# A Mamba mixer between two half feed-forward layers on one core: order in the first block, roots ahead of states, four banks for turned rows, the two closing items joined, the last product in two parts

## The chip, the cores and the metric

One core of a Trainium2 chip. The metric is the device time of one launch in microseconds (us), as the median of several runs. Engines are named as in the profile: PE (matmuls), PEld (its weight loads), DVE, ACT, POOL, and SP, which here only issues DMAs. The clock of PE has two levels, 1.2 and 2.4 GHz; the profile gives the share that is granted.

## What is computed

The input is 4 batches of 512 tokens with 512 features, in fp32. Three layers follow one another, each with a residual:

```
x = x + 0.5 * ffn(layernorm(x))
x = x + mixer(layernorm(x))
x = x + 0.5 * ffn(layernorm(x))

ffn:   h = fwht(x * SU_ug) / 64
       up   = h @ W_up.T   * scale      (512 -> 2048)
       gate = h @ W_gate.T * scale
       h = fwht(silu(gate) * up * SU_dp) / 64
       return h @ W_down.T * scale      (2048 -> 512)
mixer: gate, xBC, dt = split(x @ in_proj.T)        (512 -> 1024 + 1280 + 64)
       xBC = silu(causal conv of width 4 over time)
       state-space scan in chunks of 64 tokens: 64 heads of 16, state 128
       y = rmsnorm((y + D x) * silu(gate)) @ out_proj.T
```

Both feed-forward layers use the same weights. The Walsh-Hadamard transforms (fwht) are folded into the weights by the kernel itself in its opening part.

## The kernel before, in words

**Precision.** A product of two fp32 matrices is made as three passes over high and low halves (fp32r), so 128 x 128 weights against 512 columns are three matmuls, and a projection over 512 features is 12. Where rows come out of an engine, ACT writes the high half (a copy) and DVE the low half (a subtraction).

**Opening part** (`begin`, to about 363 us): it transforms the weights and runs the first feed-forward layer for batches 0 and 1. The change doesn't touch it.

**Items.** `mixer` then runs six items, q = 0 to 5. In items 0 to 3 the mixer of batch q runs, and beside it a feed-forward layer of another batch, `beside(q)`: the first layer of batches 2 and 3, then the second of 0 and 1. Items 4 and 5, the closing ones, are feed-forward alone, the second layer of batches 2 and 3. Every item has eight blocks, b = 0 to 7; `at` = 8 q + b counts them. A block of the feed-forward part makes 256 of the 2048 hidden features: `gate0`, `up0`, `gate1`, `up1` (12 matmuls each), then `down`, four tiles t of 6 matmuls each, added to `res` by DVE (`add_down`). A mixer's block makes 128 of the 1024 inner features: `in_proj` twice, a transpose (`x_rows`), decays (`decay`, four per block, each followed by an exponential on ACT into `L` and a product with `GT`, three by DVE and one by POOL, the last), chunk states (`new_states` on PE, then the recurrence `states` on DVE in 13 steps), `times_start`, the products `ydiag` and `from_states`, and per two blocks `out_proj`.

**Order.** Each engine has an order written out by hand, and engines wait on semaphores. What is ahead on an engine holds up what is behind it. Around the change:
- PE, block b > 0 of a mixer: `x_rows`, `decay` 0, `down` 0 and 1 of the block before, `decay` 1, `down` 2, `decay` 2, `down` 3, `decay` 3, `in_proj`, `new_states`, `times_start`, `up0`, `gate1`, `ydiag`, `from_states`, `in_proj(q, 6 + 2b)`, `up1`, then `out_proj` or directly `gate0` of the next block. `in_proj(q, 6 + 2b)` waits for `conv` (on bank PB).
- DVE in the same block: `scaled`, additions and products in turn, `times_g(2)`, `states`, `conv` (three dependent steps), `hidden(at, 0)`, `hidden_low(at, 0)`, `within`, `carried`, then at b = 4 the second half of the layer norm's statistics (`roots`, 22 steps on 128 x 4 elements, and `bias`) for the feed-forward side, and at b = 6 of items 0 to 2 the same for the mixer's side, then `hidden(at, 1)` and `hidden_low(at, 1)`. `down(at, 0)` of PE waits for the latter.
- POOL: the product of the fourth decay (`times_g`), `low_part` and `add_squares` of the block before, `combine` (two operations on `y`, after `carried`).
- At the end of an item the normalized rows of the next one are turned: ACT writes a row tile to one of two slots of `xn` (`beside_row`), PE transposes it into a bank S[0] or S[1] in turn (`beside_turn`, between the tiles of `down`), ACT copies the high half to `fxT`, DVE subtracts the low half. The third turn waits until the first low half is out of its bank.
- In the first block of mixer 0 ACT runs `end_decays` (exponential), `x_silu` and `gate` (both silu), then exponentials again.
- After the last block the item's `down` is done for both halves j of the hidden features at once, tile by tile, in the two banks F.
- SP issues all loads in one queue; after item 4 it writes the item's rows out, each tile after its addition, and only then issues the loads of item 5 from its second on.

Of the kernel before, what the change touches and what calls it, by code (L numbers as in the profile page):

```python
# [18 lines left out]
F32 = mybir.dt.float32  # L19
# [808 lines left out]
def mixer(nc, s, ug_s, dn_s, wsc, in_s, out_s, cum_m, cum_s, out):  # L828
# [17 lines left out]
    with ExitStack() as ctx:  # L846
# [55 lines left out]

        def beside(q):

            return (q + 2) % BATCH
# [139 lines left out]
        def _(pe):  # L1045
# [43 lines left out]
            def beside_turn(i, t):  # L1089

                pe.wait_ge(s_fxn, TPG * (i - 1) + t + 1)
                if t >= 2:
                    pe.wait_ge(s_fxlo, TPG * (i - 1) + t - 1)
                elif t == 0:
                    pe.wait_ge(s_z, NB * min(i, BATCH))
                    wait(pe, s_v, i - 1 if i > BATCH else 0)
                    wait(pe, s_fxlo, TPG * (i - 1) - 1)
                else:
                    pe.wait_ge(s_st, NB * min(i, BATCH))
                    wait(pe, s_fxlo, TPG * (i - 1))  # L1100
                for k in range(KH):
                    ins = pe.transpose(S[t % 2][:, ck(k)], xn[:, t % 2, ck(k)], I)
                ins.then_inc(s_ftr, 1)

            def half_up(n, to, ks=range(KH)):

                w, loaded, count = up_slot(n)
                if ks[0] == 0:
                    pe.wait_ge(loaded, count)
                    wait(pe, s_fxlo, TPG * (n // (4 * NC)))  # L1110
                for k in ks:
                    for i, (a, b) in enumerate(PASSES):
                        ins = pe.matmul(to[:], w[:, a, k, :], fxT[:, b, k, :], start=(k == 0 and i == 0), stop=(k == KH - 1 and i == 2))  # L1113
                return ins

            def gate0(at, pairs):
# [3 lines left out]
                elif at % NC:  # L1120
                    pe.wait_ge(s_sil, 2 * at)
                else:
                    wait(pe, s_acc, TPG * at)
# [6 lines left out]
            def gate1(at):  # L1130
                if at % NC:
# [8 lines left out]
            def down(at, t, pairs=0):  # L1140
# [7 lines left out]
                elif t == 1:  # L1148
                    pe.wait_ge(s_sil, 2 * at + 2 if at % NC == NC - 1 else 2 * at + 3)
# [5 lines left out]
                ins.then_inc(s_d, 1)  # L1155

# [101 lines left out]
            def ends_out(q):  # L1258

                pe.wait_ge(s_dg, q + 1)  # L1260
                pe.wait_ge(s_cv, LCONV * q + 2)
                wait(pe, s_L, QUADS * NB * q)
# [27 lines left out]
            for q in range(BATCH):  # L1290
                more = q < BATCH - 1
                for b in range(NB):
# [5 lines left out]
                    if b == 0:  # L1298
                        if q:
                            up0(at)  # L1300
# [67 lines left out]
            for q in range(BATCH, ITEMS):  # L1368
                for b in range(NB):
                    at = NC * q + b  # L1370
                    pair = last_pair(q, b)
                    if b:
                        down(at - 1, 0, last_pair(q, b - 1) + 1)
                        down(at - 1, 1)
                    if q == BATCH and b == 1:
                        sums(q - 1)
                    if b:
                        down(at - 1, 2)
                        down(at - 1, 3)
                    up0(at)  # L1380
                    gate1(at)
                    up1(at)
                    if pair >= 0:
                        out_proj(pair, at)
                    if b < NB - 1:
                        gate0(at + 1, pair + 1)
                if q < ITEMS - 1:
                    beside_turn(q + 1, 0)
                    down(at, 0)
                    beside_turn(q + 1, 1)  # L1390
                    down(at, 1)
                    beside_turn(q + 1, 2)
                    down(at, 2)
                    beside_turn(q + 1, 3)
                    down(at, 3)
                    gate0(at + 1, 0)
                else:
                    for t in range(TPG):
                        down(at, t)

        @block.scalar
        def _(act):
# [37 lines left out]
            def beside_turn(i, t):  # L1440
                act.wait_ge(s_ftr, TPG * (i - 1) + t + 1)
                act.wait_ge(s_u, 2 * NC * i)
                act.copy(fxT[:, 0, :, ck(t)], S[t % 2][:].rearrange("p (k n) -> p k n", k=KH)).then_inc(s_fxhi, 1)
# [73 lines left out]
            def beside_row(i, t):  # L1517

                act.wait_ge(s_fs, i)
                act.wait_ge(*((s_tr, TPG * min(i, BATCH - 1)) if t < 2 else (s_ftr, TPG * (i - 1) + t - 1)))  # L1520
                act.activation(xn[:, t % 2, :], tiles(beside(i))[t], ACT.Identity, bias=mv[:, 1, 1, t:t + 1],
# [33 lines left out]
            b_rows(0)  # L1555
            end_decays(0)
            x_silu(0, 0)
            gate(0, 0)
# [61 lines left out]
            for q in range(BATCH, ITEMS):  # L1620
                for b in range(NB):
                    at = NC * q + b
                    if q == BATCH and b == 0:
                        high(q - 1, NB - 1)
                    hidden_high(at, 0)
                    if q == BATCH and b == 0:
                        square(q - 1, NB - 1)
                    silu(at, 1)
                    hidden_high(at, 1)
                    if b < NB - 1:  # L1630
                        silu(at + 1, 0)
                if q < ITEMS - 1:
                    beside_row(q + 1, 0)
                    beside_row(q + 1, 1)
                    beside_turn(q + 1, 0)
                    beside_row(q + 1, 2)
                    beside_turn(q + 1, 1)
                    beside_row(q + 1, 3)
                    beside_turn(q + 1, 2)
# [456 lines left out]
```

## Time and profile before

| what | us |
|---|---|
| median of three runs | 1694.22 |
| lowest and highest of them | 1693.03, 1702.69 |
| the profiled execution, its own time | 1699.64 |
| its span in the profile | 1697.5 |
| granted clock, mean share | 0.991 |
| time of PE's order: opening part, to | 363 |
| mixers and the layers beside them, to about | 1414 |
| closing items, to | 1697.5 |

The profile is of one execution. A timeline row gives a start, the time that the instructions of the group took together, engine and line, and in brackets how long the engine was idle before it and what ended that. Matmuls are pipelined: twelve in a row take 2.7 to 3.0 us while a single one is listed with 0.39.

### The profile page before, as it was taken

To read this page: it belongs to the slowest core of one execution; us is meant where nothing else is said; L and a number is where in the kernel's file an instruction comes from. 1 tells how busy PE (TensorE), PEld (TensorE's weight loads), DVE (VectorE), ACT (ScalarE), POOL (GpSimd) and SP (SyncE) were. 2 spreads that over 40 slices of the span, in tenths; PEclk is the share of its full clock that TensorE was granted. 3 is DMA by queue.
4 is the path that set the end of the run, shared out by engine and by line. 5 is a ranking of instruction groups with operands and counts; after the bars stand their busy time and mean duration, and the time that the engine had idled before them with its cause. 6 is when DMAs were issued, how large, how long until landed. Compare 5 with 4: busy or idle time off the path is not lost.

```text
span 1697.5 us, 25014 instructions
## 1 busy us (share of the span) xinstructions
PE 1633.7 (96%) x9672; PEld 1317.8 (78%) x9672; DVE 1032.5 (61%) x2022; ACT 630.3 (37%) x936; POOL 378.4 (22%) x298
## 2 busy tenths in 40 slices
PE   6899999898999999999999999999999999999998
PEld 3677777676888877888877888877888887887886
DVE  6634444576667676677777777677677664443333
ACT  4333333345333355234355333345343332112111
POOL 3356662011212112122222131221222130000000
PEclk9999999999999999999999999999999999999999
DMA  8656654454445535545444445445444447566563
GB/s 254 235 187 235 227 200 180 184 175 144 155 151 165 162 113 169 170 143 174 152 144 153 147 163 162 163 139 186 142 163 158 157 127 221 164 191 191 179 206 112
DMA packets 253427, 290.46 MB, mean 171 GB/s; under 512 B 14464, under 2 KB 211200, under 8 KB 244096
## 3 DMA queue, kind: packets, MB, share of 16 engines
q1 hardware_dynamic: 253312, 288.88, 51.8%
q8 instruction: 78, 1.28, 0.3%
q14 instruction: 37, 0.30, 0.1%
HBM read 238.51 MB, written 50.33 MB: 170 GB/s over the span
## 4 chain that ended last, share of the span: by engine, by line
PE 62%; DVE 11%; ACT 3%; issue 2%; POOL 0%; DVEq 0%; ACTq 0%; POOLq 0%
PE bank L1113 25%; PE bank L1154 14%; PE bank L1076 10%; PE bank L1170 4%; PE bank L1239 2%; DVE m_cv L1696 2%; PE bank L1226 2%; PE bank L1188 1%; DVE m_sta L1740 1%; PE bank L1210 1%; DVE m_sta L1742 1%; DVE xn L1669 1%; PE bank L1198 1%; DVE m_mv L164 1%; ACT m_hb L1455 1%
## 5 line engine op out<-in xcount | busy, mean ns | idle before, releaser
L1113 PE MATMUL bank<-fxT,wj 128*128 128x512 f32 x1992 | 471.2, 390 | 2.3 <-DVE fxT L1662 1.5
L1113 PEld LDWEIGHTS bank<-fxT,wj 128*128 128x128 f32 x1992 | 373.8, 188 | 80.9 <-DVE res L1681 3.1
L1154 PE MATMUL bank<-m_wd,m_hb 128*128 128x512 f32 x1152 | 287.6, 395 | 6.6 <-DVE m_hb L1675 6.2
L1154 PEld LDWEIGHTS bank<-m_wd,m_hb 128*128 128x128 f32 x1152 | 214.2, 189 | 54.1 <-issue 11.7
L1076 PE MATMUL bank<-xT,wi 128*128 128x512 f32 x912 | 227.1, 397 | 3.2 <-DVE m_cv L1696 2.1
L1455 ACT CAST m_hb<-xn 128x512 fp32r<-128x512 f32 x96 | 59.5, 620 | 449.8 <-DVE xn L1669 449.8
L1076 PEld LDWEIGHTS bank<-xT,wi 128*128 128x128 f32 x912 | 169.0, 189 | 41.5 <-issue 5.8
L1681 DVE TENSOR_TENSOR res<-bank,res 128x512 f32<-128x512 f32 x192 | 132.5, 690 | 90.8 <-PE bank L1154 89.9
L1994 POOL TENSOR_TENSOR m_L<-m_L,m_GT 128x512 f32<-128x512 f32 x36 | 52.8, 1468 | 459.4 <-ACT m_L L1464 459.4
L1669 DVE SCALAR_TENSOR_TENSOR xn<-bank,sc,xn 128x512 f32<-128x512 f32 x96 | 71.7, 747 | 131.0 <-PE bank L1113 130.9
L1449 ACT ACTIVATE xn<-bank,sc 128x512 f32<-128x512 f32 x96 | 66.0, 688 | 141.0 <-PE bank L1113 137.5
L1464 ACT ACTIVATE m_L<-bank 128x512 f32<-128x512 f32 x128 | 76.5, 598 | 100.5 <-PE bank L1188 100.2
L518 PE MATMUL bank<-b_wd,b_hb 128*128 128x512 f32 x384 | 96.7, 402 | 12.1 <-DVE res L726 11.8
L1675 DVE TENSOR_TENSOR m_hb<-xn,m_hb 128x512 fp32r<-128x512 f32 x96 | 66.3, 690 | 54.9 <-ACT m_hb L1455 54.9
L518 PEld LDWEIGHTS bank<-b_wd,b_hb 128*128 128x128 f32 x384 | 71.9, 191 | 33.5 <-DVE res L726 18.4
L1696 DVE SCALAR_TENSOR_TENSOR m_cv<-bank,pr,m_cv 128x511 f32<-128x511 f32 (+2 forms) x120 | 89.5, 746 | 12.3 <-ACT m_cv L1409 9.5
L496 PE MATMUL bank<-xT,b_wu 128*128 128x512 f32 x384 | 96.4, 400 | 0.0
L496 PE MATMUL bank<-b_xT,b_wu 128*128 128x512 f32 x384 | 93.9, 394 | 0.0
L1170 PE MATMUL bank<-m_wo,m_yh 128*128 128x512 f32 x384 | 90.8, 392 | 0.7 <-ACT xn L1449 0.7
L496 PEld LDWEIGHTS bank<-xT,b_wu 128*128 128x128 f32 x384 | 72.4, 189 | 17.9 <-issue 0.7
L1170 PEld LDWEIGHTS bank<-m_wo,m_yh 128*128 128x128 f32 x384 | 71.7, 188 | 17.7 <-issue 1.9
L496 PEld LDWEIGHTS bank<-b_xT,b_wu 128*128 128x128 f32 x384 | 72.1, 188 | 17.0 <-issue 1.9
(210 smaller groups left out, 2169.7 us busy)
## 6 DMA issues: line engine op xcount, KB each, us to landing
wj<-ug_split SPq DMA_DIRECT2D x167, 512.0 KB, 4.2
m_wd<-dn_split SPq DMA_DIRECT2D x48, 1024.0 KB, 4.9
wi<-in_split SPq DMA_DIRECT2D x76, 512.0 KB, 3.3
ug_split<-b_wu SPq DMA_DIRECT2D x8, 2048.0 KB, 14.2
m_wo<-out_split SPq DMA_DIRECT2D x32, 512.0 KB, 4.1
wi<-ug_split SPq DMA_DIRECT2D x25, 512.0 KB, 4.2
in_split<-b_msp SPq DMA_DIRECT2D x20, 512.0 KB, 3.7
raw<-in_wug SPq DMA_DIRECT2D x8, 1024.0 KB, 7.0
```

The source lines that it names most:

```text
L496: ins = pe.matmul(U[j][:], wu[c % 2][:, a, k, ck(j)], xT[g][:, b, k, :], start=(k == 0 and i == 0), stop=(k == KH - 1 and i == 2))
L518: ins = pe.matmul(D[t % 2][:], hb[:, n % 2, a, j, ck(t)], wd[c % 2][:, b, j, :], start=(j == 0 and i == 0), stop=(j == 1 and i == 2))
L1076: ins = pe.matmul(to[:], w[:, a, k, :], xT[:, b, k, :], start=(k == 0 and i == 0), stop=(k == KH - 1 and i == 2))
L1113: ins = pe.matmul(to[:], w[:, a, k, :], fxT[:, b, k, :], start=(k == 0 and i == 0), stop=(k == KH - 1 and i == 2))
L1154: ins = pe.matmul(F[t % 2][:], hb[:, a, j, ck(t)], wd[:, b, j, :], start=(j == 0 and n == 0), stop=(j == 1 and n == 2))
L1170: ins = pe.matmul(F[1 - t % 2][:], yh[:, (2 * pair + i) % 4, a, ck(t)], wout[i][:, b, :], start=(i == 0 and n == 0), stop=(i == 1 and n == 2))
L1455: act.copy(hb[:, 0, j, :], hf[:, j, :]).then_inc(s_hi, 1)
L1464: act.activation(L[:, b % 2, j, :], A[:], ACT.Exp).then_inc(s_L, 1)
L1669: dve.scalar_tensor_tensor(hf[:, j, :], F[0][:], sc[:, at % NC, 2 + j:3 + j], hf[:, j, :], ALU.mult, ALU.mult).then_inc(s_h, 1)
L1675: dve.tensor_tensor(hb[:, 1, j, :], hf[:, j, :], hb[:, 0, j, :].bitcast(F32), ALU.subtract).then_inc(s_lo, 1)
L1681: dve.tensor_tensor(r, F[t % 2][:], r, ALU.add).then_inc(s_acc, 1)
L1696: ins = dve.scalar_tensor_tensor(cv[:, d:SEQ], frm[:, 0:SEQ - d], pr[:, w + 3 - d:w + 4 - d], cv[:, d:SEQ], ALU.mult, ALU.add)
```

## The change

It does five things.

1. First block of mixer 0: ACT runs `gate` and `x_silu` ahead of `end_decays`; PE runs `decay` 0, half of `in_proj(0, 5)`, `decay` 1 and 2, the other half, `decay` 3, and `new_states` last.
2. On DVE the `roots` and `bias` steps at b = 4 (items 0 to 3) and b = 6 (items 0 to 2) stand right ahead of `states`, no longer behind `carried`. In closing item 4 they stay.
3. Turned rows at the end of a mixer go to four banks (S[0], S[1], A, X), so that none waits for another's low half. `products` and `ends_out` of the next mixer, which use X and A, wait for the low halves instead.
4. Closing items are one loop over `at`: `gate0` of item 5 follows item 4 as inside an item, ahead of `down`. The rows of item 5 are written in block 5 of item 4 (four tiles of `L` as slots), turned in block 6 between `gate1` and `up1` into four banks, and copied to `xT` (free by then) after the next `silu`; DVE subtracts the low halves at the end of block 6.
5. The last `down` goes first over all four tiles for j = 0, then for j = 1, in four banks (PB, A, X, Y).

```diff
+        def beside_bank(i, t):
+            return (S[0], S[1], A if i <= BATCH else Y, X)[t]
+        def beside_to(i):
+            return fxT if i < ITEMS - 1 else xT
+        def opens(at):
+            return at % NC == 0 and at < NC * (ITEMS - 1)
+        def closes(at):
+            return at % NC == NC - 1 and at != NC * (ITEMS - 1) - 1
+        def beside_tile(i, t):
+            return xn[:, t % 2, :] if i < ITEMS - 1 else L[:, 0, t, :]
+        def end_bank(t):
+            return (PB, A, X, Y)[t]
...
             def beside_turn(i, t):
+                mixed = min(i, BATCH)
                 pe.wait_ge(s_fxn, TPG * (i - 1) + t + 1)
-                if t >= 2:
-                    pe.wait_ge(s_fxlo, TPG * (i - 1) + t - 1)
+                if i == ITEMS - 1:
+                    pe.wait_ge(s_v, BATCH)
+                    pe.wait_ge(s_fxlo, TPG * (i - 1))
                 elif t == 0:
-                    pe.wait_ge(s_z, NB * min(i, BATCH))
-                    wait(pe, s_v, i - 1 if i > BATCH else 0)
-                    wait(pe, s_fxlo, TPG * (i - 1) - 1)
+                    pe.wait_ge(s_z, NB * mixed)
+                elif t == 1:
+                    pe.wait_ge(s_st, NB * mixed)
+                elif t == 2:
+                    pe.wait_ge(s_L, QUADS * NB * mixed)
                 else:
-                    pe.wait_ge(s_st, NB * min(i, BATCH))
-                    wait(pe, s_fxlo, TPG * (i - 1))
+                    pe.wait_ge(s_ex, NB * mixed)
...
+            def down_last(at):
+                pe.wait_ge(s_wd, 16 * (at + 1))
+                for j in range(2):
+                    pe.wait_ge(s_hi, 2 * at + j + 1)
+                    pe.wait_ge(s_lo, 2 * at + j + 1)
+                    for t in range(TPG):
+                        for n, (a, b) in enumerate(PASSES):
+                            ins = pe.matmul(end_bank(t)[:], hb[:, a, j, ck(t)], wd[:, b, j, :], ...)
+                        if j:
+                            ins.then_inc(s_d, 1)
...
             def products(q):
                 pe.wait_ge(s_xcv, LCONV * q + 2)
-                wait(pe, s_ex, NB * q)
+                wait(pe, s_fxlo, TPG * q)
...
                     decay(q, b, 0)
-                    if b == 0:
-                        if q:
-                            up0(at)
+                    if at == 0:
+                        in_proj(q, 5, 0)
+                        decay(q, b, 1)
+                        decay(q, b, 2)
+                        in_proj(q, 5, 1)
+                        decay(q, b, 3)
+                        new_states(q, b)
+                    elif b == 0:
+                        up0(at)
...
+            for at in range(NC * BATCH, NC * ITEMS):
+                q, b = at // NC, at % NC
+                pair = last_pair(q, b)
+                if not opens(at):
+                    down(at - 1, 0, last_pair(q, b - 1) + 1 if b else 0)
+                    down(at - 1, 1)
...
+                    down(at - 1, 2)
+                    down(at - 1, 3)
+                up0(at)
+                gate1(at)
+                if q == BATCH and b == 6:
+                    for t in range(TPG):
+                        beside_turn(q + 1, t)
+                up1(at)
+                if pair >= 0:
+                    out_proj(pair, at)
+                if at < NC * ITEMS - 1:
+                    gate0(at + 1, pair + 1)
+            down_last(NC * ITEMS - 1)
...
             b_rows(0)
+            gate(0, 0)
+            x_silu(0, 0)
             end_decays(0)
-            x_silu(0, 0)
-            gate(0, 0)
...
+                    if b == 4:
+                        next(other)
+                        bias(1, s_fs)
+                    if b == 6 and more:
+                        next(following)
+                        bias(0, s_ms)
                     states(q, b)
...
-                    if b in (3, 4):
+                    if b == 3:
                         next(other)
-                    if b == 4:
-                        bias(1, s_fs)
-                    if b in (5, 6) and more:
+                    if b == 5 and more:
                         next(following)
-                    if b == 6 and more:
-                        bias(0, s_ms)
```

## Rows read from the trace of the kernel before

**Rows 1.** The page, busy time of the engines: us, share of the span, instructions.

```profile
PE 1633.7 (96%) x9672; PEld 1317.8 (78%) x9672; DVE 1032.5 (61%) x2022; ACT 630.3 (37%) x936; POOL 378.4 (22%) x298
```

**Rows 2.** Timeline of PE, block b=4 of mixer 0: start, us, instructions [idle before].

```profile
521.15 3.01 PE L1076 MATMUL bank<-xT,wi 128*128 128x512 f32 x12
523.99 5.61 PE L1113 MATMUL bank<-fxT,wj 128*128 128x512 f32 x24
...
530.73 1.62 PE L1154 MATMUL bank<-m_wd,m_hb 128*128 128x512 f32 x6 [0.45 <-DVE m_hb L1675]
```

**Rows 3.** Timeline of DVE in the same block.

```profile
509.28 0.68 DVE L1727 TENSOR_TENSOR m_L<-m_L,m_GT 128x512 f32<-128x512 f32 x1
512.74 0.29 DVE L1736 COPY m_sta<-bank 128x128 f32<-128x128 f32 x1 [2.78 <-PE bank L1226]
...
516.86 2.31 DVE L1696 SCALAR_TENSOR_TENSOR m_cv<-bank,pr,m_cv 128x511 f32<-128x511 f32 x3
...
522.31 0.15 DVE L159 TENSOR_TENSOR m_mv<-m_st 128x4 f32<-128x4 f32 x1
...
522.65 1.01 DVE L162 TENSOR_SCALAR m_mv<-m_mv 128x4 f32<-128x4 f32 x1
...
523.76 1.25 DVE L164 SCALAR_TENSOR_TENSOR m_mv<-m_mv 128x4 f32<-128x4 f32 x1
...
528.35 0.75 DVE L1669 SCALAR_TENSOR_TENSOR xn<-bank,sc,xn 128x512 f32<-128x512 f32 x1
```

**Rows 4.** Timeline of POOL in the same block.

```profile
509.57 1.54 POOL L1994 TENSOR_TENSOR m_L<-m_L,m_GT 128x512 f32<-128x512 f32 x1 [17.40 <-ACT m_L L1464]
511.07 1.28 POOL L2015 TENSOR_TENSOR m_yh<-m_y,m_yh 128x512 fp32r<-128x512 f32 x1
...
522.47 1.17 POOL L2009 TENSOR_TENSOR m_y<-m_y,m_ex 128x448 f32<-128x448 f32 x1
523.72 1.28 POOL L2011 TENSOR_TENSOR m_y<-m_y,m_zs 128x512 f32<-128x512 f32 x1
```

**Rows 5.** Timeline of POOL and DVE, block b=0 of mixer 1.

```profile
656.59 1.31 POOL L1994 TENSOR_TENSOR m_L<-m_L,m_GT 128x512 f32<-128x512 f32 x1 [17.12 <-ACT m_L L1464]
...
657.09 0.94 DVE L1740 TENSOR_TENSOR m_sta<-m_sta,m_dc 128x128 f32<-128x128 f32 x1
```

**Rows 6.** Timeline of DVE, closing item 4, block b=4.

```profile
1494.04 0.16 DVE L159 TENSOR_TENSOR m_mv<-m_st 128x4 f32<-128x4 f32 x1
...
1498.13 0.75 DVE L1669 SCALAR_TENSOR_TENSOR xn<-bank,sc,xn 128x512 f32<-128x512 f32 x1
```

**Rows 7.** Timeline of PE, end of mixer 0.

```profile
632.02 0.63 PE L1102 MATMUL bank<-cs,xn 128*128 128x128 f32 x4 [0.89 <-DVE fxT L1662]
```

**Rows 8.** Timelines of PE and ACT between the closing items, of DVE after mixer 3.

```profile
1412.19 1.28 DVE L1662 TENSOR_TENSOR fxT<-bank,fxT 128x512 fp32r<-128x512 f32 x2
...
1548.63 1.52 ACT L1521 ACTIVATE xn<-res,m_mv 128x512 f32<-128x512 f32 x2
...
1549.49 0.66 PE L1102 MATMUL bank<-cs,xn 128*128 128x128 f32 x4 [2.28 <-ACT xn L1521]
...
1558.50 2.99 PE L1113 MATMUL bank<-fxT,wj 128*128 128x512 f32 x12 [1.47 <-DVE fxT L1662]
```

**Rows 9.** The end: timeline of PE, then the stretches view (PEclk before DMA share).

```profile
1687.05 7.28 PE L1154 MATMUL bank<-m_wd,m_hb 128*128 128x512 f32 x24 [2.49 <-DVE m_hb L1675]
...
1688.00:1690.00 2.00, 2.00 (x7) 1.54 (x7) 0.69 (x1) 0.00 (x0) 0.00 (x0) 0.56 0.00 0
```

**Rows 10.** First block of mixer 0: timeline, then the stretches view.

```profile
390.33 1.28 ACT L1464 ACT_TABLE_LOAD   x1
...
395.99 2.07 PE L1226 MATMUL bank<-m_xd,m_Bt 64*128 64x128 f32 x14
...
405.41 3.01 PE L1076 MATMUL bank<-xT,wi 128*128 128x512 f32 x12 [0.54 <-DVE m_cv L1696]
...
392.00:394.00 2.00, 1.72 (x4) 1.44 (x5) 1.96 (x5) 0.82 (x2) 0.00 (x0) 0.50 0.00 0
```

More of the change, by code:

```diff
@@ L1939, in _ @@
                     keep_rows(q + 1)
-            for q in range(BATCH, ITEMS):
-                other = stats(beside(q + 1), 1) if q < ITEMS - 1 else None
-                for b in range(NB):
-                    at = NC * q + b
-                    pair = last_pair(q, b)
-                    if b:
-                        add_down(at - 1, 0)
-                        add_down(at - 1, 1)
+            other = stats(beside(ITEMS - 1), 1)
+            for at in range(NC * BATCH, NC * ITEMS):
+                q, b = at // NC, at % NC
+                pair = last_pair(q, b)
+                if not opens(at):
+                    add_down(at - 1, 0)
+                    add_down(at - 1, 1)
@@ L1948, in _ @@
                     if q == BATCH and b == 1:
                         keep_sums(q - 1)
-                    if b:
-                        add_down(at - 1, 2)
-                        add_down(at - 1, 3)
-                    hidden(at, 0)
-                    hidden_low(at, 0)
-                    if q == BATCH and b == 1:
-                        norm(q - 1)
-                    if q == BATCH and b == 2:
-                        ending(q - 1)
-                    if other and b in (3, 4):
-                        next(other)
@@ L1961, in _ @@
-                    if other and b == 4:
-                        bias(1, s_fs)
-                    hidden(at, 1)
-                    if pair >= 0:
-                        add_out(pair, 0)
-                    hidden_low(at, 1)
-                    if pair >= 0:
-                        for t in range(1, TPG):
-                            add_out(pair, t)
-                for t in range(TPG):
-                    add_down(at, t)
-                    if other:
+                    add_down(at - 1, 2)
@@ new lines, in _ @@
+                    add_down(at - 1, 3)
+                hidden(at, 0)
+                hidden_low(at, 0)
+                if q == BATCH and b == 1:
+                    norm(q - 1)
+                if q == BATCH and b == 2:
+                    ending(q - 1)
+                if q == BATCH and b in (3, 4):
+                    next(other)
+                if q == BATCH and b == 4:
+                    bias(1, s_fs)
+                hidden(at, 1)
+                if pair >= 0:
+                    add_out(pair, 0)
@@ L1973, in _ @@
+                hidden_low(at, 1)
+                if pair >= 0:
+                    for t in range(1, TPG):
+                        add_out(pair, t)
+                if q == BATCH and b == 6:
+                    for t in range(TPG):
                         beside_turn(q + 1, t)
+            for t in range(TPG):
+                add_down(NC * ITEMS - 1, t)
         @block.gpsimd
```

106 lines of the change are left out of this document (42 added, 64 removed).

## The prediction

> **What bounds the kernel now.** I read the page first. PE is busy 96% of the span [rows 1] and the granted clock is full in all forty slices, so the body is a string of matmuls and only stretches in which PE waits can be won: 63.8 us in all, most of them in the opening part, which the change leaves alone. Then I went through PE's timeline from 363 us on for the rows with an idle time in brackets, and at each of them through the timelines of all engines. What the change can touch is:
> - seven waits of 0.45 to 0.46 us ahead of the first down product of a block, one after block b=4 of each of the four mixers (530.73, 793.89, 1057.10, 1320.36) and one after b=6 of the first three (592.04, 855.21, 1118.39). One stands in [rows 2]; the reader is to see that it ends on the low half of the hidden rows;
> - three waits of 0.89 us at the end of the first three mixers, for a bank of the turned rows [rows 7];
> - 2.28 and 1.47 us between the two closing items [rows 8];
> - 2.49 us ahead of the last product, after which the granted clock falls [rows 9];
> - the first block of the first mixer, where PE waits several times and from 392 to 398 us runs at 0.50 of its clock, 1.2 GHz [rows 10].
>
> Idle of the seven, three, two and one together: 3.2 + 2.7 + 3.75 + 2.5 = 12.1 us of 1697.5. That is the ceiling apart from clock and first block, and it is 0.7%.
>
> **Part by part. Roots ahead of states.** The 22 little steps of roots and the one of bias stand now between carried and hidden(at, 1), and take 528.35 - 522.31 = 6.04 us there [rows 3]. The same chain in the closing item, where POOL does nothing, takes 1498.13 - 1494.04 = 4.09 us [rows 6]. The difference is two steps of 1.01 and 1.25 us instead of 0.17, and they end where POOL's two operations on y end (522.47 + 1.17 and 523.72 + 1.28) [rows 3, 4]. So DVE stands still while POOL has hold of something both want. That is seen with another operation too: the product with the decays took 0.94 us beside POOL, where it otherwise takes 0.29 [rows 5].
>
> In the new place the chain starts when times_g(2) is through, at 509.28 + 0.6 = 509.9, and is meant to fill the 2.78 us in which DVE waits for the new states [rows 3]. It is 4.09 us long even undisturbed, so states starts at 514.0 and not 512.74. But POOL runs times_g(3) and low_part back to back exactly there, until 511.07 + 1.28 = 512.35 [rows 4]. If both hold DVE up, the chain runs after them: 512.35 + 4.09 = 516.4, and states is 516.4 - 512.74 = 3.7 us late. What is late next: conv comes 4.12 us after the start of states and takes 2.31 [rows 3], and in_proj(q, 6 + 2b) on PE waits for it. Before, it was ready at 519.17 and PE came at 521.15 [rows 2]: a spare of 1.98. So PE stalls 3.66 - 1.98 = 1.68 us (about 1 of it already ahead of from_states) and gets back the 0.45: net +1.23, seven times +8.6. The queue behind is up1 and all that follows on PE, with no slack to take it up. hidden(at, 1), now without roots ahead of it, is on time.
>
> Bounds: nothing held up, start 514.0, late by 1.24 and under the spare, so -0.45 seven times, -3.2. One of POOL's two only: some 515.2, stall 0.5, about 0. The top: both, and the spare smaller by a semaphore's way of 0.15, +9.7. I take +8.6, since POOL's two operations lie in 509.8 to 512.35 in the very stretch and the rows show DVE waiting through whole ones.
>
> The Trainium skill speaks against this move as well: SBUF — State Buffer, section "Who interferes with whom", has a VectorE instruction with two SBUF inputs, or in a 2-port mode, and a GpSimd instruction that reads SBUF exclude each other for a whole instruction, the one issued first going first. The held-up steps fit that [rows 3 to 5]. Read to the letter, the first three steps, issued before low_part, would slip in between POOL's two and start the rest 0.3 us sooner: by the page the sum would be some 2 us lower.
>
> **Four banks for turned rows.** At the end of mixers 0 to 2 the third turn no longer waits for the low half of the first [rows 7]: 3 x 0.89 = 2.7 us. Its row of xn and the sum on bank F that the down product needs are there by then, so nothing else holds it. New waits: products(q+1) now waits for all four low halves, of which the last stands behind run_sums on DVE; PE has a projection of 12 matmuls before it, and I put the spare at about 1 us. If it is gone, the 0.9 is given back: -2.7 to 0. At the end of mixer 3 PE waits for sums on F, not for these banks, and nothing changes. I take -2.7.
>
> **Closing items joined.** 2.28 + 1.47 = 3.75 us go [rows 8]: gate0(40) now lies ahead of down(39), as inside an item. The sixteen transposes are as many as before, now in one go at b=6. Four rows on ACT at b=5 take twice 1.52 us [rows 8], while PE does the 12 matmuls of up1, and fit. A new wait comes at b=6: on DVE the four subtractions stand ahead of add_down(38, 0). After gate0(39) come silu and the first copy, some 0.7 each (estimate), then four subtractions at 0.64 [rows 8] and an addition of 0.69: 1.4 + 2.6 + 0.6 = 4.6 us, where PE wants bank F[0] after twelve matmuls, half of 5.45 [rows 2], at 2.7. Stall 1.9. Net -1.9, between -3.75 (no stall) and 0. SP's four writes of the item's rows now wait while PE goes on, and the load_up behind them is needed only some 12 us later: nothing.
>
> **Last product in two parts.** The first half of the sum over j needs nothing of hidden 1, so its twelve matmuls fill the 2.49 us [rows 9]; 12 take 2.7. The four banks free it from the additions. The 24 matmuls took 7.28 us there against 5.61 elsewhere [rows 9, 2], since the clock granted fell to 0.56 after the wait; without the wait it should stay: 1.6 more. Together -4.1; without the clock -2.5.
>
> **First block.** gate and x_silu ahead of end_decays save two of the table loads of 1.28 us [rows 10], and the first decay_exp starts about 1.4 us sooner. But new_states, done at 395.99 + 2.07 = 398.06 before, now comes after all four decays and the second half of in_proj(0, 5). With the clock at half there as before, I count decay 0.5, exponent 0.6 and the way between for each: new_states is done at about 398.3. One collision of states with times_g(3) goes, 0.7. So in_proj(0, 6) starts at about 404.9, not 405.41: -0.5. At full clock it would be 402.7, -2.7. On the other side PE then waits nearly 3 us for states, and if the clock falls again after that for as long, some 7 us of matmuls cost 3.4 more: +0.8. I take -0.5: the clock fell there before, and the wait ahead of the fall becomes shorter but stays.
>
> **Sum.** +8.6 - 2.7 - 1.9 - 4.1 - 0.5 = -0.6 us. Against the profiled execution that is a span of 1696.9 for 1697.5, and 1699.0 for its time of 1699.64. The median of the runs is 1694.22, 5.4 lower; the same difference gives 1693.6.
>
> **The rivals.**
> 1. Roots are hidden: POOL and the small steps pass one another. For it: the operands have four columns, and some steps beside POOL did run in 0.15. Against it: 1.01 and 1.25 in the very chain. Then -3.2 in place of +8.6: -12.4, 1681.8.
> 2. In between: one of POOL's operations holds the chain up, about 0 for the roots, -9.2: 1685.
> 3. Slower: each new stall of 1.7 us (in two pieces, of 1.1 and 0.6) brings the clock to half for some 7 us, as the 2.49 us did for 3.4 us. A stretch of 7 us of matmuls costs 3.4 more, seven times 24: 1717.6. For it: rows 9. Against it: 2.28 us of waiting at 1549.49 brought no fall. It decides as soon as the clock falls at five of the seven.
> 4. The gains at the banks and at the join don't come, since DVE's order (additions and subtractions in turn) and not the bank sets the pace: +2.7 and +1.9 on the sum, 1698.2.
>
> **How the numbers follow.** Forecast 0.6, rival 1 0.14, rival 2 0.12, rival 3 0.05, rival 4 0.09. A measurement of this kernel tells about 1% from no change, 17 us; all but rival 3 lie within. The range reaches from rival 1 to rival 4: 1681 to 1699. The forecast's own is 1690 to 1697. Slower by over 1%: rival 3, 0.05. Faster by over 1%, under 1677.3: rival 1 with the first block at full clock and the join free, 0.03.
>
> **What would show it.** In the profile after: at b=4 and b=6 the steps of roots right after times_g(2), two of them of about a microsecond, states starting over 3 us after PE's new states, and PE idle ahead of from_states and of the projection, seven times. No waits at L1154 of 0.45. At the mixers' ends no 0.89. At the join one wait of 1.9 for the sum on F. At the end no gap, full clock and four products 0.7 us apart. The forecast is wrong if roots takes 4.1 us in its new place, or if it takes 6 and the projection still starts without a wait.

## The result and the profile after

The changed kernel takes 1704.86 us (median of ten runs, 1697.93 to 1707.44), the kernel before 1697.42 beside it (ten runs). The ratio is 1.0038, 95% interval 1.0020 to 1.0056: 6.5 us slower, where 0.6 us faster was forecast (1693.6, range 1681 to 1699). It is clear of noise, though under the 1% that the chances went by. The forecast in absolute time stood on a median of 1694.22 for the kernel before, which beside the changed kernel took 1697.42: of the 11.3 us between 1693.6 and 1704.86, 3.2 belong to the kernel before and not to the change. Taken as differences, the range went from 13.2 us faster to 4.8 slower. The 6.5 lies outside, while its interval (3.4 to 9.5) reaches in.

The profiled execution has a span of 1701.3 us. In it the opening part, which the change doesn't touch, ended 2.7 us sooner than in the one of before (361.13 against 363.81), so the spans differ by 3.8 and the stretch from there to the end by 6.5. That stretch is what is compared from here on. Cut at points that both kernels have (all from PE's timeline, in us):

| from ... to | before | after | difference |
|---|---|---|---|
| start of mixer 0 ... first down product | 50.57 | 52.58 | +2.0 |
| ... products of mixer 1 | 224.17 | 227.09 | +2.9 |
| ... products of mixer 2 | 263.17 | 266.03 | +2.9 |
| ... products of mixer 3 | 263.20 | 266.07 | +2.9 |
| ... sums of mixer 3 (block 1 of item 4) | 265.71 | 268.18 | +2.5 |
| ... end of the last up product | 253.77 | 251.38 | -2.4 |
| ... end | 13.11 | 8.86 | -4.3 |

Every mixer became slower, and both closing parts faster. Four views of the changed kernel show how. First PE's timeline at b=4 and b=6 of mixer 0 (start, us, instructions, idle before and what ended it), the answer to [rows 2]:

```profile
519.72 1.78 PE L1279 MATMUL bank<-m_Cf,m_sta 128*128 128x64 f32 x14 [0.75 <-DVE m_sta L1783]
522.03 4.57 PE L1100 MATMUL bank<-xT,wi 128*128 128x512 f32 x12 [0.54 <-DVE m_cv L1737]
...
583.46 1.77 PE L1279 MATMUL bank<-m_Cf,m_sta 128*128 128x64 f32 x14 [0.75 <-DVE m_sta L1783]
585.77 3.00 PE L1100 MATMUL bank<-xT,wi 128*128 128x512 f32 x12 [0.54 <-DVE m_cv L1737]
```

The wait of 0.45 us is gone, and two have come in its place, 0.75 ahead of from_states and 0.54 ahead of the projection, at all seven places. The twelve matmuls at 522.03 take 4.57 us, the same twelve at 585.77 take 3.00. The stretches view tells why (us; then busy time of PE, PEld, DVE, ACT, POOL with instructions; granted clock of PE; DMA share; GB/s):

```profile
520.00:522.00 2.00, 1.49 (x14) 1.35 (x13) 1.93 (x4) 0.00 (x0) 0.00 (x0) 1.00 0.80 240
522.00:524.00 2.00, 1.97 (x5) 1.62 (x6) 1.32 (x3) 1.41 (x3) 0.20 (x1) 0.52 0.00 0
524.00:526.00 2.00, 2.00 (x8) 1.57 (x7) 1.11 (x2) 1.99 (x3) 1.90 (x2) 0.63 0.04 8
...
585.00:587.00 2.00, 1.46 (x8) 1.14 (x7) 1.31 (x3) 0.68 (x2) 0.00 (x0) 1.00 0.15 40
```

After the pair of waits at b=4 the clock is at half, 1.2 GHz, for 3.4 us (522.1 to 525.5), at b=6 it isn't. It is so in all four mixers of this execution (at b=6 in the three that have the pair there); in the one of before the clock is full from 398 us to 1688.

DVE in the same block, the answer to [rows 3], and POOL, to [rows 4]:

```profile
508.62 0.68 DVE L1768 TENSOR_TENSOR m_L<-m_L,m_GT 128x512 f32<-128x512 f32 x1
509.21 1.25 DVE L159 TENSOR_TENSOR m_mv<-m_st 128x4 f32<-128x4 f32 x1
510.39 0.15 DVE L160 TENSOR_TENSOR m_mv<-m_st 128x4 f32<-128x4 f32 x1
510.46 1.25 DVE L161 TENSOR_TENSOR m_mv<-m_st 128x4 f32<-128x4 f32 x1
511.75 0.17 DVE L162 TENSOR_SCALAR m_mv<-m_mv 128x4 f32<-128x4 f32 x1
...
515.47 0.29 DVE L1777 COPY m_sta<-bank 128x128 f32<-128x128 f32 x1
...
519.58 2.31 DVE L1737 SCALAR_TENSOR_TENSOR m_cv<-bank,pr,m_cv 128x511 f32<-128x511 f32 x3
```

```profile
508.91 1.54 POOL L2036 TENSOR_TENSOR m_L<-m_L,m_GT 128x512 f32<-128x512 f32 x1 [17.39 <-ACT m_L L1503]
510.41 1.28 POOL L2057 TENSOR_TENSOR m_yh<-m_y,m_yh 128x512 fp32r<-128x512 f32 x1
```

The first step of roots waits out the product with GT on POOL, the third waits out low_part: 1.25 us each instead of 0.15. The chain takes 515.47 - 509.21 = 6.26 us where it was meant to take 4.09 [rows 6] and to fill 2.78. The recurrence starts 3.4 us after PE's new states are there (PE finished them at 512.05). In the kernel before it started 0.03 us after them (512.71 and 512.74).

The end of item 4 and the end of the kernel, the answers to [rows 8] and [rows 9], from the timelines of PE, ACT and DVE:

```profile
1545.63 2.92 PE L1182 MATMUL bank<-m_wd,m_hb 128*128 128x512 f32 x12
1546.42 2.04 ACT L1482 CAST xT<-bank 128x512 fp32r<-128x512 f32 x4
1547.03 2.48 DVE L1702 TENSOR_TENSOR xT<-bank,xT 128x512 fp32r<-128x512 f32 x4 [1.72 <-ACT xT L1482]
1549.43 1.28 DVE L1722 TENSOR_TENSOR res<-bank,res 128x512 f32<-128x512 f32 x2
1550.16 3.02 PE L1182 MATMUL bank<-m_wd,m_hb 128*128 128x512 f32 x12 [1.62 <-DVE res L1722]
...
1692.46 5.63 PE L1193 MATMUL bank<-m_wd,m_hb 128*128 128x512 f32 x24
```

2.28 and 1.47 us have become one wait of 1.62, for the first addition, which stands behind four subtractions. The last 24 matmuls run in 5.63 us with nothing ahead of them, where they took 7.28 behind a gap of 2.49.

### The profile page after: what moved, and what is told of

It is laid out like the page before. It is cut to its first block, busy times and chain, and to the rows that moved or that the text cites. A ratio compares the mean times of both kernels' runs of the same rounds, so it can differ in the third digit from the quotient of the medians.

```text
span 1701.3 us, 25015 instructions
## 1 busy us (share of the span) xinstructions
PE 1641.5 (96%) x9672; PEld 1323.3 (78%) x9672; DVE 1031.6 (61%) x2022; ACT 627.8 (37%) x934; POOL 378.6 (22%) x298
## 3 DMA queue, kind: packets, MB, share of 16 engines
q8 instruction: 78, 1.28, 0.3%
## 4 chain that ended last, share of the span: by engine, by line
PE 66%; DVE 9%; ACT 1%; issue 1%; DMA 0%; SPq 0%; ACTq 0%; DVEq 0%
PE bank L1141 27%; PE bank L1182 14%; PE bank L1100 11%; PE bank L1210 5%; PE bank L1279 2%; PE bank L1228 1%; DVE m_sta L1781 1%; DVE m_cv L1737 1%; PE bank L1250 1%; PE bank L1266 1%; DVE m_sta L1783 1%; PE bank L1238 1%; DVE res L1722 1%; PE bank L1273 1%; DVE m_mv L161 0%
## 5 line engine op out<-in xcount | busy, mean ns | idle before, releaser
L1141 PE MATMUL bank<-fxT,wj 128*128 128x512 f32 x1764 | 417.9, 391 | 0.8 <-DVE res L1722 0.8
L1141 PEld LDWEIGHTS bank<-fxT,wj 128*128 128x128 f32 x1764 | 331.0, 188 | 70.2 <-DVE res L1722 1.2
L1182 PE MATMUL bank<-m_wd,m_hb 128*128 128x512 f32 x1128 | 279.5, 393 | 2.5 <-DVE res L1722 1.6
L1182 PEld LDWEIGHTS bank<-m_wd,m_hb 128*128 128x128 f32 x1128 | 209.1, 188 | 47.7 <-issue 3.7
L1100 PE MATMUL bank<-xT,wi 128*128 128x512 f32 x912 | 235.6, 409 | 6.7 <-DVE m_cv L1737 5.6
L1100 PEld LDWEIGHTS bank<-xT,wi 128*128 128x128 f32 x912 | 175.3, 196 | 48.0 <-issue 9.9
L518 PE MATMUL bank<-b_wd,b_hb 128*128 128x512 f32 x384 | 97.2, 403 | 11.3 <-DVE res L726 11.0
L2063 POOL TENSOR_TENSOR m_ss<-m_ss,m_y 128x512 f32<-128x512 f32 x28 | 36.1, 1290 | 238.3 <-ACT m_y L1523 238.3
```

The source lines that it names most:

```text
L518: ins = pe.matmul(D[t % 2][:], hb[:, n % 2, a, j, ck(t)], wd[c % 2][:, b, j, :], start=(j == 0 and i == 0), stop=(j == 1 and i == 2))
L1100: ins = pe.matmul(to[:], w[:, a, k, :], xT[:, b, k, :], start=(k == 0 and i == 0), stop=(k == KH - 1 and i == 2))
L1141: ins = pe.matmul(to[:], w[:, a, k, :], frm[:, b, k, :], start=(k == 0 and i == 0), stop=(k == KH - 1 and i == 2))
L1182: ins = pe.matmul(F[t % 2][:], hb[:, a, j, ck(t)], wd[:, b, j, :], start=(j == 0 and n == 0), stop=(j == 1 and n == 2))
```

## Experiments

Each kernel is compared with runs of the kernel before on the same chip. Ratios have their 95% interval; a difference in us is the ratio times 1697 to 1700.

### Roots back behind carried

```diff
-                    if b == 4:
-                        next(other)
-                        bias(1, s_fs)
-                    if b == 6 and more:
-                        next(following)
-                        bias(0, s_ms)
                     states(q, b)
...
-                    if b == 3:
+                    if b in (3, 4):
                         next(other)
-                    if b == 5 and more:
+                    if b == 4:
+                        bias(1, s_fs)
+                    if b in (5, 6) and more:
                         next(following)
+                    if b == 6 and more:
+                        bias(0, s_ms)
```

> The changed kernel with roots and bias back behind carried in the mixers; the other four parts stay. Theory A, roots ahead of states is what costs: the waits ahead of from_states (0.75 us) and of the projection (0.54) go and those of 0.45 return, 0.84 us seven times, 5.9, and the falls of the clock at b=4 go with them, up to 6.8 more. So 6 to 13 us below the changed kernel, and some 6 us below the kernel before (banks -2.7, join -2.1, last product -4.1, first block +2.6). Theory B, another part costs (the first block, the join): within 2 us of the changed kernel. In the profile A wants no stretch at half clock between 410 us and the end.

Measured: 0.9955 (0.9938 to 0.9971), 7.6 us faster than before and so 14 us faster than the changed kernel. The pairs of waits are gone, those of 0.45 are back (0.46 to 0.50 here), and from 416 us to the end of PE's work no stretch at half clock is left. The last one before, 412.5 to 415.9 us, is that of the first block, which in this execution starts 9 us later than in the changed kernel's. From products to products an item takes 262.16 us (mean of two), against 266.03 with roots ahead and 263.17 before: 1.0 less than before, which is the banks' part. Theory A holds, with a gain 1 us above its range; B falls.

### Roots ahead of states and nothing else

```diff
+                    if b == 4:
+                        next(other)
+                        bias(1, s_fs)
+                    if b == 6 and more:
+                        next(following)
+                        bias(0, s_ms)
                     states(q, b)
...
-                    if b in (3, 4):
+                    if b == 3:
                         next(other)
-                    if b == 4:
-                        bias(1, s_fs)
-                    if b in (5, 6) and more:
+                    if b == 5 and more:
                         next(following)
-                    if b == 6 and more:
-                        bias(0, s_ms)
```

> The kernel before with roots and bias ahead of states in the mixers and nothing else changed. Theory A: 6 to 13 us above the kernel before, with the same pairs of waits of 0.75 and 0.54 at b=4 and b=6. Theory B: within 2 us of the kernel before. Whether the clock falls at b=4, at b=6 or at none is open; if it falls after the pair of waits at some blocks, each fall of 3.4 us at half clock costs 1.7.

Measured: 1.0072 (1.0057 to 1.0087), 12.2 us slower. The same pairs of 0.75 and 0.54 stand at all seven places. In its profile the clock falls after three of them, at b=6 of mixer 0 and at b=4 of mixers 1 and 3. That separates the two costs. The item from the products of mixer 2 to those of mixer 3 has two pairs and no fall and takes 265.53 us against 263.20 before, 2.3 more; the one ahead of it has two pairs and one fall, and takes 267.17 against 263.17, 4.0 more. So a pair costs 1.2 us net of the wait that it replaces (the two waits less 0.45, and 0.3 in small waits and in starting up again behind them), and a fall of the clock 1.6 to 1.7. Roots alone cost 12.2 us and the other four parts alone gain 7.6. That adds up to 4.6, beside 6.5 measured for all five, each of the three with an interval of 2.5 to 3 us to either side.

It shows the end of the kernel too: the wait of 2.49 us is there, but the clock stays full, and the 24 matmuls take 5.68 and not 7.28.

```profile
1699.16 5.68 PE L1154 MATMUL bank<-m_wd,m_hb 128*128 128x512 f32 x24 [2.49 <-DVE m_hb L1675]
```

### POOL writes and doesn't read

```diff
-                pool.tensor_tensor(yh[:, b % 4, 1, :], y[:, b % 2, :], yh[:, b % 4, 0, :].bitcast(F32), ALU.subtract).then_inc(s_yl, 1)
+                pool.memset(yh[:, b % 4, 1, :].bitcast(F32), 0.0).then_inc(s_yl, 1)
```

> The changed kernel, but POOL's low_part is a fill with zeros (it writes and reads nothing), so the low halves of y are left out of out_proj. Theory C, DVE is held up by POOL's reads of SBUF: L159 is still held up by the product with GT for 1.25 us, L161 no longer, so the chain takes 5.0 and not 6.26 us, states starts 1.2 us sooner, the wait ahead of from_states goes and the one ahead of the projection is under 0.1, with no fall of the clock at b=4. Rival: the chain is slow in that place for another reason, or the fill holds DVE up as well: 5.5 to 6.3 us.

Measured in a single execution: 1690.43 us. DVE's and POOL's timelines of that kernel at b=4:

```profile
511.94 1.25 DVE L159 TENSOR_TENSOR m_mv<-m_st 128x4 f32<-128x4 f32 x1
513.12 0.15 DVE L160 TENSOR_TENSOR m_mv<-m_st 128x4 f32<-128x4 f32 x1
513.19 0.15 DVE L161 TENSOR_TENSOR m_mv<-m_st 128x4 f32<-128x4 f32 x1
513.38 0.28 DVE L162 TENSOR_SCALAR m_mv<-m_mv 128x4 f32<-128x4 f32 x1
...
517.17 0.29 DVE L1777 COPY m_sta<-bank 128x128 f32<-128x128 f32 x1
```

```profile
511.64 1.54 POOL L2036 TENSOR_TENSOR m_L<-m_L,m_GT 128x512 f32<-128x512 f32 x1 [17.40 <-ACT m_L L1503]
513.11 0.52 POOL L2057 MEMSET m_yh<- 128x512 f32 x1
```

L159 is held up for 1.25 us as before by the product with GT; L161 starts beside the fill and takes 0.15, not 1.25. The chain takes 5.23 us. The wait ahead of from_states is gone at all seven places, and one of 0.33 to 0.35 is left ahead of the projection (expected under 0.1: the chain was 0.2 longer than the 5.0 expected). No fall of the clock after 410 us. So what held DVE up is POOL's operation that reads SBUF, shown for low_part by putting one in its place that only writes, and for the product with GT by its place alone. The edit changes the kind of the operation and its length (0.52 us, not 1.28) together with the reading, and no run takes these apart. The Trainium skill, SBUF — State Buffer, section "Who interferes with whom", says of a VectorE instruction with two SBUF inputs that it contends with a GpSimd instruction that reads SBUF, "not with one that only writes it"; the trace agrees (L161 ran wholly beside the fill, in 0.15). L162, a tensor_scalar, took 0.28 instead of 0.17 and ended with the fill. The same section counts tensor_scalar among the operations that can enter a 2-port mode and contend there; that fits, but no view shows in which mode L162 ran.

### One Newton step less

```diff
-    for _ in range(4):
+    for _ in range(3):
         ch.step(eng.tensor_tensor(t, y, y, ALU.mult))
```

> Like the kernel with roots back behind carried, but rsqrt runs three Newton steps and not four, so the chain is three instructions of 0.2 us shorter everywhere. If the waits of 0.45 us after b=4 and b=6 come from the length of the chain behind carried, all eight of them (the closing item's with them) go: 3.5 us below the kernel with roots back. If they come from the hidden rows' own way (silu, product, copy, subtraction), nothing changes.

Measured: 0.9933 (0.9917 to 0.9949), 11.4 us faster than before, 3.7 below the kernel with roots back. All eight waits of 0.45 are gone: the chain in its old place was too long by less than these 0.6 us. The two intervals overlap; in the profiles the stretch from mixer 0 to the end is 1322.67 us against 1326.31 with four steps, 3.6 less. What roots ahead of states was to win is had without moving it. But this edit changes what is computed: it leaves out the last step of each rsqrt, so its gain isn't one of order alone.

### The first block as before

On top of three Newton steps.

```diff
-                    if at == 0:
-                        in_proj(q, 5, 0)
-                        decay(q, b, 1)
-                        decay(q, b, 2)
-                        in_proj(q, 5, 1)
-                        decay(q, b, 3)
-                        new_states(q, b)
-                    elif b == 0:
-                        up0(at)
+                    if b == 0:
+                        if q:
+                            up0(at)
...
-            gate(0, 0)
-            x_silu(0, 0)
             end_decays(0)
+            x_silu(0, 0)
+            gate(0, 0)
```

> The kernel with three Newton steps, and the first block of mixer 0 as it was before on ACT and on PE. From the start of mixer 0 to the first down product the kernel before took 50.6 us and the kernels with the new first block 52.6 to 53.0. Theory D, the new order costs there: 2.2 us faster than the kernel with three Newton steps, and one fall of the clock less. Rival, the 2 us come from something else that differs (loads, phase of the clock): no difference.

Measured: 0.9924 (0.9895 to 0.9953), 12.9 us faster than before; the 1.5 us to the kernel with three Newton steps lie inside the intervals. In the profile the block took 51.88 us against 52.91, not the 50.57 of before, since in this execution the clock fell a second time, from 400.9 to 407.7 us. Direction as expected, size half, and the fall not saved. The order of before is thus in three profiles, and without a second fall in one of them only: 50.57 us in the kernel before, 51.85 with roots alone, 51.88 here. With the new order the block takes 52.58 to 52.95 us in five profiles and 54.15 in a sixth.

### ACT's new order with PE's old one

```diff
-                    if at == 0:
-                        in_proj(q, 5, 0)
...
-                    elif b == 0:
-                        up0(at)
+                    if b == 0:
+                        if q:
+                            up0(at)
```

> The kernel with three Newton steps, with ACT's new order in the first block (gate, x_silu, end_decays) and PE's order as before. Theory D1, the loss comes from new_states at the end of PE's order, which starts the 13 steps of states late, while ACT's order gains: two table loads of 1.28 us less, so 49.2 us to the first down product and 3 us or more below the kernel with three Newton steps. Rival, ACT's order is what costs: 52 us or more.

Measured: 0.9906 (0.9884 to 0.9929), 16 us faster than before. The first down product comes 48.66 us after the start of the mixer, 4.2 sooner than with PE's new order and 1.9 sooner than before. So ACT's order gains and PE's loses, as theory D1 has it. A part of the 4.2 is the clock: with PE's new order the first stretch at half clock in this block is 10.2 us long in all six profiles and a second one always follows, with PE's old order the first is 6.8 in all five, and with ACT's new order beside it there is no second. The two timelines side by side, first the changed kernel (mixer 0 starts at 361.13), then this one (at 362.18):

```profile
386.81 0.77 PE L1228 MATMUL bank<-m_mvg,m_stn 128*128 128x512 f32 x1 [0.97 <-ACT m_dc L1585]
387.66 2.93 PE L1100 MATMUL bank<-xT,wi 128*128 128x512 f32 x6
390.39 0.63 PE L1228 MATMUL bank<-m_mvg,m_stn 128*128 128x512 f32 x1
...
395.41 1.31 PE L1266 MATMUL bank<-m_xd,m_Bt 64*128 64x128 f32 x14
...
401.32 2.11 PE L1279 MATMUL bank<-m_Cf,m_sta 128*128 128x64 f32 x14 [2.54 <-DVE m_sta L1783]
```

```profile
387.86 0.77 PE L1228 MATMUL bank<-m_mvg,m_stn 128*128 128x512 f32 x1 [1.07 <-ACT m_dc L1579]
389.31 0.79 PE L1228 MATMUL bank<-m_mvg,m_stn 128*128 128x512 f32 x1 [0.69 <-ACT m_L L1497]
...
393.02 1.53 PE L1266 MATMUL bank<-m_xd,m_Bt 64*128 64x128 f32 x14
```

In the changed kernel the second decay stands behind six matmuls of the projection, which take 2.93 us at half clock, and starts 29.3 us after the mixer's start; with PE's old order it starts at 27.1. New states starts at 34.3 there and at 30.8 here. DVE's 13 steps and the projection behind them follow.

### Subtractions spread at the join

```diff
                 if not opens(at):
                     add_down(at - 1, 0)
+                    if turns:
+                        beside_turn(q + 1, 0)
                     add_down(at - 1, 1)
+                    if turns:
+                        beside_turn(q + 1, 1)
...
-                if q == BATCH and b == 6:
-                    for t in range(TPG):
-                        beside_turn(q + 1, t)
```

> The kernel with three Newton steps, with the four subtractions of the turned rows of item 5 put one behind each add_down of block 7 and no longer ahead of the first. The wait of 1.6 us between the closing items comes from add_down standing behind four subtractions: it goes, 1.6 us faster. An addition and a subtraction take 1.2 us together and a tile of down 1.37, so no new wait.

Measured: 0.9921 (0.9898 to 0.9944), against 0.9933 without it. The wait of 1.6 us is gone and no other has come: from the sums of mixer 3 to the last up product it takes 248.84 us instead of 250.84. The intervals of the two ratios are wider than these 2 us, so only the profile shows them. (From mixer 0 to the end the two profiles differ by 0.65 us only, since the first block took 1.2 longer here, 54.15 us, its second stretch at half clock being 6.8 us and not 3.4.)

### The changed kernel once more

> The changed kernel once more, unaltered. If the clock falls by the place of the two waits alone, it falls again after those at b=4 in all four mixers and at no b=6. If it depends on how the waits happen to lie against something that runs on its own, the falls are elsewhere this time, or their number differs from four, between 0 and 7, each worth 1.7 us.

Measured in a single execution: 1703.63 us, span 1701.5. The pairs of waits are the same to 0.02 us. The clock falls after three of them: at b=4 of mixers 0 and 1, and at b=6 of mixer 2. PE's timeline and the stretches view (as above) at the last of the three, where the first profile has full clock:

```profile
1118.10 4.58 PE L1100 MATMUL bank<-xT,wi 128*128 128x512 f32 x12 [0.54 <-DVE m_cv L1737]
...
1118.00:1120.00 2.00, 1.90 (x5) 1.54 (x6) 1.32 (x3) 1.34 (x3) 0.13 (x1) 0.55 0.13 33
```

So the falls aren't bound to a place in the kernel, as the expectation's second reading has it. What decides between one pair and the next isn't settled: the waits are equal, and no view shows what the fall goes by. The falls within one execution needn't be independent either: in the first profile the four at b=4 come 266.24 us apart each, while the items are 266.03 to 266.07 long, so they may be one coincidence seen four times.

### What points to a faster kernel, together

The changed kernel with four of the edits above: roots back, three Newton steps, PE's old order in the first block, and the subtractions spread.

```diff
-    for _ in range(4):
+    for _ in range(3):
...
-                    if at == 0:
-                        in_proj(q, 5, 0)
...
-                    if b == 4:
-                        next(other)
...
-                if q == BATCH and b == 6:
-                    for t in range(TPG):
-                        beside_turn(q + 1, t)
```

> The changed kernel with what the runs so far point to: roots and bias back behind carried, three Newton steps, ACT's new order in the first block with PE's old one, and the subtractions of item 5 spread over the additions of block 7. If the parts add up, 48.7 us to the first down product, no wait between the closing items, and from the start of mixer 0 to the end 1318.6 - 1.6 = 1317.0 us in the profile; 16 to 18 us below the kernel before in the medians. If spreading only moves the wait, 1318.6.

Measured: 1679.67 us, 0.9884 (0.9865 to 0.9903), 19.7 us faster than before and 26 us faster than the changed kernel (16 to 18 below the kernel before were expected). The first down product comes after 48.79 us, there is no wait between the closing items, and from the start of mixer 0 to the end it is 1316.71 us: the parts add up. The Newton step that is left out has its share in this.

## Why the prediction was wrong, and where it was right

By the stretch from mixer 0 to the end, each term of the sum:

| term | forecast | in the profile |
|---|---|---|
| roots ahead of states, waits | +8.6 | +8.1 |
| clock after those waits | 0 (rival 3: +24) | +6.4 |
| four banks | -2.7 | -3.0 |
| closing items joined | -1.9 | -2.4 |
| last product in two parts | -4.1 | -4.3 |
| first block | -0.5 | +2.0 |
| sum | -0.6 | +6.8 (measured +6.5) |

The roots are three items at 2.3 us and one pair at 1.2; the clock is four falls at 1.6. Both prices are those of the kernel with roots alone, and the banks are 1.0 per item from the one with roots back. The other three are differences of the table in the section on the result.

**Roots.** The mechanism was right in each step: POOL's two operations hold the chain up, the recurrence starts 3.4 us late (forecast 3.7), PE waits first for the recurrence and then for conv, 1.29 us (forecast 1.68, about 1 of it ahead of from_states). The size came out near by two errors that cancel: the wait is 0.4 shorter, and behind it come small waits at b=7 and the start-up of PE, 0.3, that weren't counted. The prediction read the rule that it cites from the Trainium skill so that the first three steps slip in between POOL's two operations. Only L160 did, L159 having waited for the first. By the starts the rule itself, that the one issued first goes first, fits: L160 starts at 510.39, low_part at 510.41 and L161 at 510.46, and L161 waits.

**Clock: the step that failed.** The sum puts the clock behind the new waits at nothing. Rival 3 named the mechanism and was given 0.05, since 2.28 us of waiting between the closing items had brought no fall [rows 8]. That compared one instance. Rival 3's own price was off too: it has 7 us at half clock behind each stall, where the fall of [rows 9] is 3.4 us long, as the ten that came were. And the prediction took the clock of before as full in all forty slices of the page, where a 9 stands for 90% or more; its mean is 0.991 in the table of that kernel. The falls come after 4, 3 and 3 of seven equal pairs of waits of 1.3 us (the changed kernel twice, roots alone), 10 of 21, each costing 1.6; in the eight profiles of kernels without these pairs (before among them) there is none between 416 us and the last product. The mean granted clock of the other executions bears the size out. It is 0.9870 over ten executions of the changed kernel and 0.9898 over nine with roots back; 0.9872 over six with roots alone and 0.9899 over fourteen of the kernel before beside them. Over some 1700 us the two differences are worth 4.7 and 4.6 us at full clock. With 1.7 us for each fall (3.4 us at half clock) that is an estimate of 2.8 and 2.7 falls more, of seven possible. The four of the profiled execution, 6.4 us, are thus above the mean. So a new wait of about a microsecond, in two pieces with light work in between, had to be priced with half a fall each, some 0.8 us beside its own length: 5.6 us in sum, and the forecast would have been 1699, or 1702 with the 1697.42 that the kernel before took beside the changed one. The row of one execution with a wait and no fall can't exclude it, as the end of the kernel shows as well: behind the same wait of 2.49 us the clock fell in one profile [rows 9] and stayed full in another.

**First block.** The forecast counted the exponents and PE's decays, each with its way, and overlooked that the second decay is now queued behind six matmuls of the projection, 2.93 us at half clock. The 1.4 us by which the first exponent comes sooner went there: new states was done 35.6 us after the start of the mixer, and not 34.5. That is 0.9 of the +2.0 by the time the next projection starts; the rest is a second fall of the clock, 402.6 to 406.0 us, behind the wait of 2.54 us for states, the case that the upper bound of +0.8 was for. Luck had a part: the same order as before took 1.3 us more in two other profiles, which have a second fall and that of before has none, so against those the new order costs 0.7. ACT's part alone is worth -1.9, as the run with PE's old order shows; PE's part costs some 4, time at half clock included.

**Banks, join, last product.** As forecast, by the mechanism and within 0.5 us: the waits of 0.89 are gone, and 2.28 and 1.47 have become 1.62 (forecast 1.9). No wait ahead of products(q+1) stands in PE's timeline, so the low halves are there in time. Part of the last product's gain was luck of the execution of before: 1.6 of the 4.3 are a fall of the clock that doesn't come every time.

**The slower side.** The ranges were worked out from waits alone, with the clock as an all-or-nothing rival (24 us); three or four falls of 1.6 us each lie between, and that is where the time came out.

## What to carry to other kernels

A wait on one engine is room for another piece of work only if that piece runs there at the speed it has elsewhere: look at what the engine beside it does in those microseconds, when that one has held it up elsewhere (here POOL, which made 4.09 us of little steps 6.26). If a chain is too long for its place by a little, shorten it before you move it: three instructions less did what the move could not, at the price of one Newton step. On a kernel that PE bounds, a new wait of a microsecond can cost more than itself, since the clock may fall behind it (1.6 us each time here, after 10 of 21 pairs). And six matmuls put ahead of the one that starts a long chain elsewhere delay that chain by their whole length, 2.93 us here.

## What was not expected of the hardware

- Equal pairs of waits, 0.75 and 0.54 us with 1.6 us of light matmuls between them, are followed by 3.4 us at half clock in 10 of 21 cases, each fall between 0.1 us ahead of the start of the next matmuls and 0.6 behind it. After 416 us and ahead of the last product, no other wait in any of the profiles is followed by a fall, not the single ones of 0.33 to 0.89 us, nor the one of 1.6, nor those of 2.28 and 1.47, which stand 9 us apart.
- Behind a gap of 2.49 us 24 matmuls took 7.28 us in one execution and 5.68 in another.
- A DVE instruction on 128 x 4 elements can last until what POOL has running ends: 0.15 us became 1.25 in the first and the third step of roots, while the one between them, which started 0.02 us ahead of POOL's next operation, took 0.15. Beside a POOL instruction that only writes, the third took 0.15.
